# A Mamba and mixture-of-experts block: the chunk's diagonal products and C with B as two 64-column halves of the TensorE array

## The chip, the cores and the metric

One core of a Trainium2 chip runs the whole program in one launch. The metric is the device time of that launch in microseconds. Times below are from repeated executions and from one execution under the hardware profiler.

## The reference, cut to what matters

The input is 32 sequences of 512 tokens, 256 wide. Each goes through layer norm, a projection with rotary embedding, RMS norm, a state-space layer, layer norm and a residual; then through a feed-forward layer with a shared part and 16 experts, layer norm and a residual. The change lies in the state-space layer, whose state has 128 columns, with 8 heads of 64 channels each:

```python
Y_diag = jnp.einsum('bcln,bcsn,bhcls,bcshp->bclhp', Cr, Br, Lmat, xdt)
Y_off = jnp.einsum('bcln,bchpn,bhcl->bclhp', Cr, states_prev, jnp.exp(Acs))
return (Y_diag + Y_off).reshape(b, l, h, p)
```

`Y_diag` is what a token l receives from the tokens s of its own chunk: the product of C at l with B at s, times the decay from s to l, times the scaled input at s. `Y_off` is what it receives from the state left by the chunks before.

## The kernel before, in words

The kernel takes chunks of 128 tokens (the reference says 64; the recurrence gives the same sums), so a sequence has NT = 4 chunks. Everything is single precision. The large products (projections and the feed-forward layer) are written as three products of rounded parts, high x high, high x low and low x high, in the 32-bit rounded type (`split_mm`, whose matmul is L1443, and `down`, L1629). The products of the state-space layer are plain full-precision matmuls on unrounded data. Transposes are matmuls with the identity (L1452, L1462, L1608).

The program is software-pipelined over sequences: one pass of the loop does the state-space layer of one sequence and the feed-forward layer of the one before. Each engine runs a list of steps that is written out by hand: `lead`, `first`, `iteration(False)`, `iteration` in a loop of 29 passes, `tail`, `drain`, `last`. No planner works at run time. PSUM banks are handed out by the lists in `PLANS`: a group such as `"a"` has three banks that are used in turn, and `slot(name)` waits until the bank's last reader has freed it. `fill` marks the last matmul of a step with a semaphore increment.

The steps that matter here, all on TensorE:

- `CB()` (line 1541 on, matmul at L1547): once for each sequence. For each chunk t it makes B times C, a 128 x 128 matrix: 128 state rows are contracted, the stationary operand is `xc[:, 4, tk]` (B, 128 tokens), the moving one `xc[:, 5, tk]` (C, 128 tokens). The four results fill one bank; ScalarE copies them to `CBs` (L863).
- `diagonal(c)` (matmul at L1575): four times for each sequence. For each of the 8 heads h it multiplies the decayed and masked matrix `seg[:, c % 2, h, :]` (128 tokens s by 128 tokens l, stationary) with `xdt[:, c % 2, hs]` (128 tokens s by 64 channels, moving). It waits for `m_ready`, which VectorE gives when it has multiplied the decays by `CBs` (`decay_CB`, L1167). The eight results, 128 x 64 each, fill one bank; VectorE reads it in `chunk_y` (L1191 or, for the first chunk, L1193).
- `from_state(c)` (L1560) and `state(c)` (L1567): one full-precision matmul of 512 moving columns each.
- `cumulate()` (L1518, L1519, L1520): once for each sequence, three small full-precision matmuls on `ad`, the decays of 32 chunk-heads. L1518 and L1519 have 128 stationary and 32 moving columns. L1520 is the other way round: `rhs` with 32 columns is stationary, `upper` with 128 moves, and the result goes to partitions 0 to 31.
- `combine_by_expert()` (L1608): four transposes with 16 stationary columns.

The diagonals and `CB` stand between other steps in TensorE's order; in `iteration`:

```python
gate(4); CB(); x_by_token(0); up(3); down(1); x_by_token(1); combine_by_expert(); down(2)
settled("c_ready"); up(4); gate(5); state(0); project_z(3, 1); diagonal(0); up(5)
from_state(1); state(1); down(3); x_by_token(2); gate(6); diagonal(1); from_state(2); up(6)
```

In the profile a matmul is two kinds of record: the load of the stationary operand (PEld, LDWEIGHTS) and the stream of the moving one (PE, MATMUL). A full-precision `nc.tensor.matmul` shows as two pairs of load and matmul, a rounded-type one and a transpose as one pair.

Of the kernel before, what the change touches and what calls it, by code (L numbers as in the profile page):

```python
# [12 lines left out]
P = 128  # L13
# [19 lines left out]
def build(nc, x, wq_t, wzx_t, conv_w, conv_b, dt_bias, a_log, d_param, npw, ngw, wo_t,  # L33
# [6 lines left out]
    with ctx:  # L40
        def sb(name, shape, dt=fp32):
            return ctx.enter_context(nc.sbuf_tensor(name, shape, dt))
# [40 lines left out]
        xc = sb("xc", [P, CB_, T])  # L83
# [3 lines left out]
        xdt = sb("xdt", [P, 2, DI])  # L87
        xdec = sb("xdec", [P, 2, DI])
        xD, ysp = sb("xD", [P, 2, DI]), sb("ysp", [P, DI])
        seg = sb("seg", [P, 2, HS, P])  # L90
# [1316 lines left out]
        def _(pe):  # L1407
# [9 lines left out]
            def slot(name):  # L1417

                part, n = way.plan.where[name]
                w = len(BANKS[part])  # L1420
                if n >= w:
                    s, k = out_of(way.plan.slots[part][n - w][0], way.plan)
                    pe.wait_ge(sem[s], now(s, k) if SEM[s][3] else k)
                elif part != "p":
                    old = way.before if part in way.before.slots else way.plan
                    s, k = out_of([slot[0] for slot in old.slots[part][n::w]][-1], old)
                    pe.wait_ge(sem[s], k)
                return way.bank(name)

            def read_out(name):  # L1430
                s, k = out_of(name, way.plan)
                pe.wait_ge(sem[s], now(s, k) if SEM[s][3] else k)

            def fill(name, ins):
                part, n = way.plan.where[name]
                ins.then_inc(sem[f"{part}_for_{way.plan.slots[part][n][1]}"], 1)
# [104 lines left out]
            def CB():  # L1541
                b = slot("CB")
                read_out("xc4")
                read_out("xc5")
                for t in range(NT):
                    tk = slice(t * P, (t + 1) * P)
                    ins = nc.tensor.matmul(b[:, tk], xc[:, 4, tk], xc[:, 5, tk], start=True, stop=True)  # L1547
                fill("CB", ins)

            def x_by_token(c):  # L1550
# [18 lines left out]
            def diagonal(c):  # L1569
                b = slot(f"yd{c}")  # L1570
                read_out(f"xt{c}")
                pe.wait_ge(sem["m_ready"], c + 1)
                for h in range(HS):
                    hs = slice(h * PD, (h + 1) * PD)
                    ins = nc.tensor.matmul(b[:, hs], seg[:, c % 2, h, :], xdt[:, c % 2, hs], start=True, stop=True)  # L1575
                fill(f"yd{c}", ins)

            def y_by_channel(c):
# [80 lines left out]
            def first():  # L1659
                begin("first", "pa")  # L1660
                consts(); weights_split(1, 2); project_z(0, 0); project_z(0, 1); project_z(1, 0)
                project_z(2, 0); project_z(1, 1); project_z(3, 0); project_x(4); project_x(5); project_x(0)
                project_z(2, 1); project_x(1); cumulate(); project_x(2); settled("ad_ready"); project_x(3)
                project_z(3, 1); x_by_token(0); CB(); x_by_token(1); B_by_token(); state(0); diagonal(0)
                state(1); from_state(1); diagonal(1); x_by_token(2); from_state(2); state(2); x_by_channel(0)
                y_by_channel(0); diagonal(2); x_by_token(3); weights_split(3); project_out(0)
                settled("a_out_ACT", "xdec_ready"); y_by_channel(1); project_q(0); project_out(1)
                from_state(3); y_by_channel(2); x_by_channel(1); diagonal(3); project_q(1); settled("xn_ready")
                settled("m_ready"); project_out(2); settled("p_out_DVE"); y_by_channel(3); h_by_channel(0)
                project_out(3); settled("p_out_ACT"); settled("a_out_DVE", "yg_ready"); h_by_channel(1)  # L1670
                settled("qn_ready")
                weights_split(*range(4, len(SPLIT)))
                assert not open_

            def iteration(g=True):
                begin("steady", "paf" + g * "g")
                project_z(0, 0); project_z(1, 0); ffn_by_channel(0); project_x(4); ffn_by_channel(1)
                if g: down(10)
                settled("ffn_in_ready"); project_z(2, 0); project_x(5)
                if g: down(11); settled("last_split")  # L1680
                logits(0); logits(1); project_z(3, 0); project_x(0); gate(0); project_x(1); up(0); project_x(2)
                gate(1); up(1); project_z(0, 1); cumulate(); gate(2); settled("ad_ready"); project_z(1, 1)
                project_x(3); up(2); gate(3); down(0); settled("acc_free"); B_by_token(); project_z(2, 1)
# [3 lines that stand above are left out]
                down(4); y_by_channel(0); gate(7); state(2); up(7); settled("xdec_ready"); diagonal(2)  # L1687
                x_by_token(3); down(5); settled("a_out_ACT"); project_out(0); x_by_channel(0); y_by_channel(1)
                gate(8); from_state(3); project_q(0); project_out(1); down(6); up(8); y_by_channel(2)
                diagonal(3); down(7); settled("m_ready"); x_by_channel(1); gate(9); settled("xn_ready")  # L1690
                project_out(2); up(9); y_by_channel(3); project_q(1); settled("yg_ready"); down(8)
                settled("p_out_DVE"); project_out(3); gate(10); settled("a_out_DVE"); up(10); h_by_channel(0)
                down(9); settled("p_out_ACT"); settled("hidden_split"); gate(11); settled("f_out_ACT")
                h_by_channel(1); up(11); settled("f_out_DVE"); settled("qn_ready")
                assert not open_

            def tail():
                begin("tail", "afg")
                project_z(0, 0); ffn_by_channel(0); project_z(0, 1); project_x(4); ffn_by_channel(1); down(10)
                settled("ffn_in_ready"); project_x(5); down(11); settled("last_split"); project_z(1, 0)  # L1700
                logits(0); logits(1); project_x(0); gate(0); project_z(2, 0); up(0); project_z(3, 0); gate(1)
                project_x(1); up(1); project_x(2); gate(2); up(2); CB(); gate(3); cumulate(); down(0)
                settled("ad_ready"); settled("acc_free"); B_by_token(); project_z(1, 1); up(3); project_x(3)
                project_z(2, 1); down(1); combine_by_expert(); gate(4); settled("c_ready"); project_z(3, 1)
                up(4); x_by_token(0); gate(5); x_by_token(1); down(2); up(5); state(0); diagonal(0); state(1)
                from_state(1); gate(6); diagonal(1); down(3); y_by_channel(0); x_by_token(2); from_state(2)
                gate(7); x_by_token(3); up(6); settled("a_out_ACT"); down(4); state(2); diagonal(2)
                project_out(0); settled("xdec_ready"); up(7); down(5); y_by_channel(1); gate(8); from_state(3)
                up(8); project_out(1); down(6); gate(9); y_by_channel(2); diagonal(3); down(7)
                settled("m_ready"); up(9); project_out(2); gate(10); y_by_channel(3); down(8)  # L1710
                settled("yg_ready"); up(10); project_out(3); gate(11); settled("a_out_DVE")
                settled("f_out_ACT"); down(9); settled("hidden_split"); up(11); settled("f_out_DVE")
                assert not open_
# [77 lines left out]
```

## Time and profile before

| | |
|---|---|
| time, median of 3 runs | 3186.76 us (3184.94, 3186.76, 3191.86) |
| profiled execution, span from first to last instruction | 3185.9 us |
| PE (matmul) | 3112.3 us busy, 98%, 19648 matmuls |
| PEld (weight load) | 2722.1 us, 85% |
| DVE (VectorE) | 2394.2 us, 75% |
| POOL (GpSimd) | 2031.2 us, 64% |
| ACT (ScalarE) | 1935.2 us, 61% |
| mean granted TensorE clock | 0.989 of 2.4 GHz |

For the profiled execution only the span is given, 0.9 us under the median of the runs; its own device time is not listed beside it. Busy PE time overstates the work, since matmuls are pipelined and a record runs on while the next one has started: the length of a matmul record includes its way through the array. The distance from one start to the next is the better measure of what an instruction takes from the engine. In the timeline, instructions of one line that follow each other are merged into a row: its start, the time from the first start to the last end, and the count behind the x.

### The profile page before, as it was taken

The numbers are of one execution on the slowest core, as the hardware profiler recorded it, in microseconds if no ns is written. First come the engines' busy times: TensorE is split into PE (matmuls) and PEld (weight loads), VectorE is DVE, ScalarE is ACT, GpSimd is POOL, SyncE is SP. The second block draws the span as 40 slices with busy tenths as digits, with TensorE's granted clock in tenths as the row PEclk, the third lists the DMA queues.
The fourth block names the chain that finished last, engine by engine and source line by source line (L and its number), as shares of the span: only waits on it lengthen the run. The fifth ranks groups of instructions, "written<-read, shape, count | busy, mean of one in ns | idle before, by whom it ended". The sixth has DMA issues, their size and how long they took to land.

```text
span 3185.9 us, 62383 instructions
## 1 busy us (share of the span) xinstructions
PE 3112.3 (98%) x19648; PEld 2722.1 (85%) x19648; DVE 2394.2 (75%) x5104; ACT 1935.2 (61%) x4149; POOL 2031.2 (64%) x2311
## 2 busy tenths in 40 slices
PE   5899999999999999999999999999999999999997
PEld 4688888888888888888888888888888888888886
DVE  5877877777777777777777777778777777777763
ACT  5565666665666556666566666656656656665562
POOL 2477666677666676656676666776666776666764
PEclk7899999999999999999999999999999999999999
DMA  3123222222222222222122222222222222222222
GB/s 123 41 68 87 73 73 67 66 66 85 73 64 64 71 73 76 80 66 58 64 86 76 76 60 66 66 86 73 73 66 66 66 86 73 64 67 69 73 74 48
DMA packets 143433, 227.33 MB, mean 71 GB/s; under 512 B 18976, under 2 KB 88352, under 8 KB 143392
## 3 DMA queue, kind: packets, MB, share of 16 engines
q1 hardware_dynamic: 126496, 210.06, 20.1%
q0 software_dynamic: 16896, 16.78, 4.0%
q8 instruction: 20, 0.33, 0.0%
q14 instruction: 21, 0.17, 0.0%
HBM read 174.87 MB, written 35.13 MB: 66 GB/s over the span
## 4 chain that ended last, share of the span: by engine, by line
PE 95%; DVE 0%; POOL 0%; ACT 0%; issue 0%; ACTq 0%; DVEq 0%; POOLq 0%
PE fpb L1443 34%; PE apb L1443 20%; PE acc L1629 17%; PE apb L1575 7%; PE apb L1452 4%; PE ppb L1443 3%; PE apb L1560 3%; PE apb L1567 2%; PE ppb L1462 2%; PE apb L1547 1%; PE fpb L1492 1%; PE fpb L1462 1%; PE fpb L1494 1%; PE fpb L1608 0%; PE apb L1520 0%; PE apb L1519 0%
## 5 line engine op out<-in xcount | busy, mean ns | idle before, releaser
L652 POOL TENSOR_TENSOR hidL<-hid,hidH 128x512 fp32r<-128x512 f32 x384 | 544.9, 1419 | 234.8 <-ACT hidH L914 226.8
L1130 DVE SCALAR_TENSOR_TENSOR xc<-apb,cw,xc 128x511 f32<-128x511 f32 (+2 forms) x576 | 427.8, 747 | 63.9 <-ACT xc L827 35.9
L1629 PE MATMUL acc<-WDH,hidH 128*128 128x256 f32 x1536 | 456.7, 297 | 4.4 <-POOLq L654 4.4
L914 ACT CAST hidH<-hid 128x512 fp32r<-128x512 f32 x384 | 236.2, 615 | 341.9 <-POOL hid L647 283.6
L1629 PE MATMUL acc<-WDH,hidL 128*128 128x256 f32 x1536 | 431.4, 281 | 0.0
L1629 PE MATMUL acc<-WDL,hidH 128*128 128x256 f32 x1536 | 430.9, 281 | 0.0
L647 POOL TENSOR_TENSOR hid<-hid,cb 128x512 f32<-128x512 f32 x256 | 347.5, 1358 | 73.2 <-DVEq L1251 42.1
L1249 DVE TENSOR_TENSOR hid<-hid,fpb 128x512 f32<-128x512 f32 x384 | 261.1, 680 | 135.6 <-PE fpb L1443 132.3
L1443 PE MATMUL fpb<-fTh,UH 128*128 128x512 f32 x768 | 335.7, 437 | 0.0
L845 ACT ACTIVATE seg<-seg,acs 128x128 f32<-128x128 f32 x1024 | 313.6, 389 | 11.5 <-ACT cb L895 5.7
L1443 PE MATMUL fpb<-fTh,GH 128*128 128x512 f32 x768 | 318.6, 415 | 0.0
L1629 PEld LDWEIGHTS acc<-WDH,hidH 128*128 128x128 f32 x1536 | 289.9, 189 | 19.9 <-issue 7.4
L1443 PE MATMUL fpb<-fTh,GL 128*128 128x512 f32 x768 | 304.1, 396 | 0.0
L1443 PE MATMUL fpb<-fTh,UL 128*128 128x512 f32 x768 | 303.9, 396 | 0.0
L903 ACT ACTIVATE hid<-fpb 128x512 f32<-128x512 f32 x384 | 228.5, 595 | 123.2 <-PE fpb L1443 83.9
L1443 PE MATMUL fpb<-fTl,UH 128*128 128x512 f32 x768 | 302.5, 394 | 0.0
L1443 PE MATMUL fpb<-fTl,GH 128*128 128x512 f32 x768 | 302.5, 394 | 0.0
L1629 PEld LDWEIGHTS acc<-WDL,hidH 128*128 128x128 f32 x1536 | 290.1, 189 | 12.7 <-issue 7.2
L1629 PEld LDWEIGHTS acc<-WDH,hidL 128*128 128x128 f32 x1536 | 289.7, 189 | 0.0
L1575 PEld LDWEIGHTS apb<-xdt,seg 128*128 128x128 f32 x2048 | 246.7, 194 | 11.9 <-issue 6.6
L1575 PE MATMUL apb<-xdt,seg 128*128 128x64 f32 x2048 | 246.1, 274 | 2.9 <-DVE seg L1167 2.8
L1167 DVE TENSOR_TENSOR seg<-seg,CBs 128x1024 f32<-128x1024 f32 x128 | 198.4, 1550 | 43.6 <-ACT seg L845 34.1
(195 smaller groups left out, 8669.6 us busy)
## 6 DMA issues: line engine op xcount, KB each, us to landing
seg<-acs_row SPq DMA_DIRECT2D x128, 512.0 KB, 4.2
cb<-c_row SPq DMA_DIRECT2D x512, 128.0 KB, 2.9
xsP<-in_x SPq DMA_DIRECT2D x32, 512.0 KB, 3.6
xc<-qrot SPq DMA_DIRECT2D x32, 512.0 KB, 3.4
xc<-in_x SPq DMA_DIRECT2D x32, 512.0 KB, 4.3
out<-xc SPq DMA_DIRECT2D x32, 512.0 KB, 3.0
out<-xn POOLq DMA_DIRECT2D x32, 512.0 KB, 6.0
ZL_loaded<-in_wzx_t SPq DMA_DIRECT2D x2, 512.0 KB, 4.4
```

The lines of the kernel that those rows point to most:

```text
L647: G.tensor_tensor(hid[:, j % 2, :], hid[:, j % 2, :], cb[:, r % 2, :], ALU.mult).then_inc(sem["routed_ready"], 1)
L652: own.do(G.tensor_tensor(hidL[:, j % 2, :], hid[:, j % 2, :], hidH[:, j % 2, :].bitcast(fp32), ALU.subtract))
L845: ins = A.activation(seg[:, c % 2, h, :], seg[:, c % 2, h, :], ACT.Exp, bias=acs[:, 0, c * HS + h:c * HS + h + 1])
L903: own.do(A.activation(hid[:, j % 2, :], way.bank(f"G{j}")[:], ACT.Silu))
L914: A.copy(hidH[:, j % 2, :], hid[:, j % 2, :]).then_inc(sem["hidden_high"], 1)
L1130: ins = V.scalar_tensor_tensor(xc[:, b, s:], src[:, 0:T - s], cw[:, b, TAPS - 1 - s:TAPS - s], xc[:, b, s:], ALU.mult, ALU.add)
L1167: V.tensor_tensor(seg[:, c % 2, :, :], seg[:, c % 2, :, :], CBs[:, c, :].unsqueeze(1).broadcast_to([P, HS, P]), ALU.mult).then_inc(sem["m_ ...
L1249: own.do(V.tensor_tensor(hid[:, j % 2, :], hid[:, j % 2, :], way.bank(f"U{j}")[:], ALU.mult))
L1443: ins = nc.tensor.matmul(dst, l, r, start=n == 0, stop=n == total - 1)
L1452: ins = nc.tensor.transpose(b[:, t * P:(t + 1) * P], src(t), ident[:])
L1575: ins = nc.tensor.matmul(b[:, hs], seg[:, c % 2, h, :], xdt[:, c % 2, hs], start=True, stop=True)
L1629: ins = nc.tensor.matmul(dst, l[:, w, tk], r[:, j, :], start=j == 0 and t % 2 == 0 and n == 0, stop=j == HB - 1 and n == 2, skip_group_che ...
```

## The change

Each matmul of `CB` and of `diagonal` becomes two. The first takes the first 64 stationary columns and writes partitions 0 to 63 of the bank, the second takes the other 64 and writes partitions 64 to 127 in the same columns. The moving operand is the same for both. The semaphore increment of `fill` stays on the last matmul. Nothing else changes.

```diff
@@ CB
                 for t in range(NT):
                     tk = slice(t * P, (t + 1) * P)
-                    ins = nc.tensor.matmul(b[:, tk], xc[:, 4, tk], xc[:, 5, tk], start=True, stop=True)
+                    for r in range(0, P, P // 2):
+                        ins = nc.tensor.matmul(b[r:r + P // 2, tk], xc[:, 4, t * P + r:t * P + r + P // 2], xc[:, 5, tk],
+                                               start=True, stop=True)
                 fill("CB", ins)
@@ diagonal
                 for h in range(HS):
                     hs = slice(h * PD, (h + 1) * PD)
-                    ins = nc.tensor.matmul(b[:, hs], seg[:, c % 2, h, :], xdt[:, c % 2, hs], start=True, stop=True)
+                    for r in range(0, P, P // 2):
+                        rows_ = slice(r, r + P // 2)
+                        ins = nc.tensor.matmul(b[rows_, hs], seg[:, c % 2, h, rows_], xdt[:, c % 2, hs],
+                                               start=True, stop=True)
                 fill(f"yd{c}", ins)
```

## Rows read from the trace of the kernel before

**Rows 1.** The page: span, busy time and forty slices of TensorE, granted clock

```profile
span 3185.9 us, 62383 instructions
...
PE 3112.3 (98%) x19648; PEld 2722.1 (85%) x19648; DVE 2394.2 (75%) x5104; ACT 1935.2 (61%) x4149; POOL 2031.2 (64%) x2311
...
PE   5899999999999999999999999999999999999997
...
PEclk7899999999999999999999999999999999999999
```

**Rows 2.** The chain that ended last: by engine (page), then by line

```profile
PE 95%; DVE 0%; POOL 0%; ACT 0%; issue 0%; ACTq 0%; DVEq 0%; POOLq 0%
...
by line: PE fpb L1443 33.7%; PE apb L1443 19.5%; PE acc L1629 17.1%; PE apb L1575 6.7%; PE apb L1452 3.8%; PE ppb L1443 2.7%; PE apb L1560 2.5%; PE apb L1567 2.5%; PE ppb L1462 1.6%; PE apb L1547 0.9%; PE fpb L1492 0.9%; PE fpb L1462 0.8%; 
```

**Rows 3.** By source line: duration min/median/max, who waited; L1575, L1547, L1520

```profile
L1575 PE MATMUL apb<-xdt,seg x2048: 217/275/446, 70.6 to 3091.2; 128*128 128x64 f32 x187
...
  DVE xdt L1191: 85.4, 63
...
L1547 PE MATMUL apb<-xc x256: 270/275/423, 63.8 to 3039.0; 128*128 128x128 f32 x128
...
L1520 PEld LDWEIGHTS apb<-upper,ad x64: 105/108/153, 53.7 to 3041.0; 128*32 128x32 f32 x64
L1520 PE MATMUL apb<-upper,ad x64: 272/296/424, 53.7 to 3041.1; 128*32 128x128 f32 x64
```

**Rows 4.** Timeline of weight loads around one diagonal (start, length, count last)

```profile
1032.53 1.87 PEld L1575 LDWEIGHTS apb<-xdt,seg 128*128 128x128 f32 x16
1034.32 0.19 PEld L1443 LDWEIGHTS fpb<-fTh,UH 128*128 128x128 f32 x1
```

**Rows 5.** Timeline of matmuls, L1560

```profile
1035.83 1.02 PE L1560 MATMUL apb<-S,xc 128*128 128x512 f32 x2
```

**Rows 6.** Timeline of matmuls around one CB

```profile
1021.85 1.05 PE L1547 MATMUL apb<-xc 128*128 128x128 f32 x8
1022.74 0.60 PE L1452 MATMUL apb<-ident,xc 128*128 128x128 f32 x4
```

**Rows 7.** Timeline around L1520: matmuls, loads, loads in a late pass

```profile
1011.15 0.41 PE L1520 MATMUL apb<-upper,ad 128*32 128x128 f32 x2
1011.48 0.50 PE L1443 MATMUL fpb<-fTh,GH 128*128 128x512 f32 x1
1011.82 0.39 PE L1443 MATMUL fpb<-fTl,GH 128*128 128x512 f32 x1
...
1010.80 0.30 PEld L1519 LDWEIGHTS apb<-ad,ones 128*128 128x128 f32 x2
1011.14 0.14 PEld L1520 LDWEIGHTS apb<-upper,ad 128*32 128x32 f32 x2
1011.48 0.19 PEld L1443 LDWEIGHTS fpb<-fTh,GH 128*128 128x128 f32 x1 [0.20 <-issue]
...
2938.80 0.30 PEld L1519 LDWEIGHTS apb<-ad,ones 128*128 128x128 f32 x2
2939.14 0.14 PEld L1520 LDWEIGHTS apb<-upper,ad 128*32 128x32 f32 x2
2939.48 0.19 PEld L1443 LDWEIGHTS fpb<-fTh,GH 128*128 128x128 f32 x1 [0.20 <-issue]
```

**Rows 8.** Timeline around L1608: matmuls, then the load behind them

```profile
1025.98 0.60 PE L1452 MATMUL apb<-ident,xc 128*128 128x128 f32 x4
1026.41 0.60 PE L1608 MATMUL fpb<-ident,gt 128*16 128x128 f32 x4
...
1026.74 0.19 PEld L1629 LDWEIGHTS acc<-WDH,hidH 128*128 128x128 f32 x1
```

**Rows 9.** The chain in order of time: one product in two successive passes

```profile
1007.33 2.81 PE fpb L1443 x12
...
1103.73 2.81 PE fpb L1443 x12
```

## The prediction

> **What bounds the kernel now.** I read the page first: its busy shares and its forty slices [rows 1]. TensorE multiplies for 98% of the span, no other engine has over 75%, and the granted clock is at its upper level, 2.4 GHz, in nearly every slice. The chain that ended last [rows 2] says the same: 95% of it is PE, of which 6.7% of the span is L1575 (the products inside a chunk) and 0.9% is L1547 (C with B). TensorE is idle for 3185.9 - 3112.3 = 74 us, nearly all of it in the first, second and last slice [rows 1], outside the steady passes. So time added to TensorE's stream moves the end one for one, and time taken from it does so until a wait appears.
>
> What sets the pace in the two places is read from the timeline. A full-precision product is two records here: 2048 matmuls at L1575 for 1024 calls, 256 at L1547 for 128 calls [rows 3]. In one diagonal [rows 4] 16 weight loads start at 1032.53 and the next line's load at 1034.32: 1.79 us, 0.112 each. The matmul of 64 moving columns needs less. From the two 512-column matmuls of L1560 [rows 5], whose starts lie 1.02 - 0.60 = 0.42 us apart, a full-precision column costs 0.82 ns, so 64 of them 0.053 us and 128 of them 0.106. L1575 is therefore **bound by weight loads** (0.112 against 0.053), and half of its streaming time is idle. CB [rows 6] runs 8 matmuls from 1021.85 to 1022.74, 0.111 each, with load and stream in balance.
>
> **The change part by part.** All waits, semaphores, buffers and the order stay. Every call becomes two calls with 64 stationary columns, one writing PSUM partitions 0 to 63 and one 64 to 127. A diagonal goes from 16 pairs (load and matmul) to 32, a CB from 8 to 16; over 32 sequences that is 128 diagonals and 32 CBs, 2048 + 256 more pairs. No DMA is added, and none of VectorE, ScalarE or GpSimd gets another instruction.
>
> *One pair.* A load of 128 columns takes 0.112 us. The only short load in a matmul of this kind is that of L1520, 32 columns [rows 3, 7]: two of them span 0.14 us and one is recorded at 0.108, so they start 0.03 us apart. Load time goes by columns, and 64 columns cost about 0.057. The stream of 64 moving columns is 0.053, that of 128 is 0.106. Both halves stream all moving columns again.
>
> *Entering and leaving.* L1520 is also the only product of this kernel that uses a part of the columns with ordinary matmuls, and its surroundings are not smooth [rows 7]. The loads of L1519 start at 1010.80 and, at 0.112 each, end at 1011.02; their last matmul streams 32 columns, 0.03 us; yet L1520's load starts only at 1011.14: **0.09 us in which nothing loads or streams**. Behind it: the second matmul starts at 1011.15 + 0.41 - 0.27 = 1011.29 (0.27 is the length of L1520's shortest matmul [rows 3]), streams 128 columns until 1011.39, and the next line's load starts at 1011.48, 0.09 us later. That load isn't hidden either: the matmul that needs it is recorded with 0.50 us instead of 0.39, 0.11 more. The same distances stand around L1520 in every pass of the loop; the last one is beside it [rows 7]. They don't stand around L1608, whose stationary operand has 16 columns but which is a transpose [rows 8]: its first matmul starts 0.43 us after the first of L1452's four, and the load of L1629 follows 0.33 us behind it, 0.11 for each of three. I take it that the array changes its division between L1519 and L1520 and back, and that each change waits until it is empty. The Trainium skill (TensorEngine Tiling (Array Packing), Key Properties) says that changing the tiling mode drains TensorE, and (Restrictions) that column tiling excludes 32-bit transposes; the trace agrees with both.
>
> No two of the 160 groups are neighbours in any of the orders written out, so each pays both changes: 0.095 empty, 0.057 for a first load that nothing covers, then at the end 0.095 and 0.11.
>
> *The body.* Here the trace has no row: nowhere do two instructions address different column halves. The bounds are (a) nothing of the two halves overlaps, (b) loads follow each other but streams may run side by side, (c) loads and streams of the halves both run side by side. With the passes in the order A1 A2 B1 B2, (c) pairs A2 with B1 and B2 with the next A1, so that n products take 2n + 1 steps.
> - Diagonal, (a) or (b): 32 x 0.057 = 1.82. With the ends 0.095 + 0.057 + 1.82 + 0.095 + 0.11 = 2.18 against 1.79: +0.39, times 128 = **+50 us**.
> - Diagonal, (c): 17 x 0.057 = 0.97, with the ends 1.33: -0.46, times 128 = -59 us.
> - CB, (b) or (c): streams of 0.111 side by side, 9 x 0.111 = 1.00, with the ends 1.36 against 0.89: +0.47, times 32 = **+15 us**.
> - CB, (a): 16 x 0.111 = 1.78, with the ends 2.13: +1.24, times 32 = +40 us.
>
> I take (b), and keep (a) and (c) as ends: every row shows loads one after another, back to back, at a rate that goes by columns alone, as one supply of weights would; the streams are the part of the array that a half leaves free. The halves' loads together still bring 2 x 64 = 128 columns a pass, which is what L1575 is bound by now. That would be -59 us where I put +50 if loads ran side by side.
>
> The Trainium skill is of two minds here. TensorE: Matmul & The Clock Gate (Weight-path perf modes) gives a wider weight path no gain for fp32, which speaks for one supply, while its page TensorEngine Tiling (Array Packing) (Key Properties) says that different tiles can execute LdWeights and Matmul in parallel. By the first the sum is +65, by the second -44. No run here shows either.
>
> *What else moves.* VectorE waits for the end of a diagonal in 63 places at L1191 alone (85 us together [rows 3]) and gets it 0.4 us later; what TensorE waits for from there (the gated y) comes after other matmuls that are just as much later, so I cost this at nothing. If that cover were gone it would be up to 0.4 us a chunk. The clock stays at its upper level: the gaps are 0.1 us, and L1520's do not change it.
>
> **Sum.** 50 + 15 = +65 us, +2.0%. The profiled execution spans 3185.9 us, 0.9 below the median of 3186.8, so I add to the median: **3252 us**. What a measurement of this kernel can tell from no change is about 0.2%, 6 us.
>
> **Rivals.**
> - *(a) Nothing overlaps*: 50 + 40, 3277 us. For it: no row has two matmuls streaming at once. Against: a half-wide stream leaves the other half of the array free. Chance 0.22.
> - *(c) The halves load and stream side by side*: -59 + 15 = -44, **3143 us**. This is the mechanism of the other sign: L1575 is load-bound, and two half loads at once cut its pace from 0.112 to 0.057 a pass. It wins as soon as the 32 pairs take less than 1.79 - 0.36 for the ends - 0.12 for a diagonal's share of CB's 15 us = 1.31 us, that is under 0.041 us a pair; above that the two changes of the array's division eat it. For it: half of the streaming time at L1575 is idle now, and the halves have no cell in common. Against: the rate of loads in every row. Some of the gain may come back as waits, since VectorE and GpSimd have 64 to 75% and 1.4 us fewer a pass to hide in. Chance 0.30.
> - *A pair of a diagonal costs 0.11 after all*, because in the divided array a load is not hidden by a matmul (0.057 + 0.053), or because TensorE isn't handed two instructions in less than the 0.111 us that are the shortest steady distance now. CB's pair costs 0.057 + 0.111. With the ends that is +2.2 and +2.1 us a group: 3530 us. Against: L1520's second load starts 0.03 us after the first, under its matmul, and its two matmuls follow at the pace of streaming alone [rows 7]. Chance 0.05. The Trainium skill (TensorE: Matmul & The Clock Gate, Packing small matmuls) has a load overlap running matmuls only where the row groups differ, and the two halves share all rows; L1520 speaks against that.
> - *The array is not emptied* (as with L1608): a diagonal then costs 1.82 + 0.057 against 1.79, and the time is 3187 to 3200. Against: L1520 in every pass. Chance 0.07.
> - The forecast (b): chance 0.36.
>
> **How the numbers follow.** 3252 is the case (b), the likeliest. Slower by over 0.2% holds (b), (a), the third and a part of the fourth: 0.66. Faster is (c): 0.30. Within 0.2%: 0.04, from the fourth. Both signs have weight, so the range reaches from (c) to (a) with a few us for the sizes of the gaps: 3138 to 3290; it leaves out the 3530 us and a (c) whose streams gain more. Given (b) alone it is 3235 to 3265: the gaps are known to 0.01 us each, 160 x 0.03, and a pair's 0.057 to 0.002, 4096 x 0.002 = 8 us.
>
> **What would show it.** In the changed profile a diagonal is one block of 32 loads of 128 rows x 64 columns, about 1.82 us from its first load to its last matmul in (b) and (a), 0.97 in (c); a CB of 16 matmuls spans 1.0 us in (b) and 1.8 in (a). Before each block the loads stop for about 0.1 us, and the first matmul behind each is 0.11 us longer than its kind, which the forms of L1443, L1452 and L1629 show in their means. The share of L1575 in the chain rises from 6.7%, and TensorE's idle time outside these gaps stays near 74 us. The prediction is wrong if a pair of a diagonal takes well under 0.05 us, if no gap stands around the blocks, or if a pass of the loop (96.4 us now, by the starts of the rows of the same kind in successive passes [rows 9]) is not about 2 us longer.

## The result and the profile after

The changed kernel takes 3138.6 us (median of 4 runs, 3134.3 to 3140.8) against 3186.6 us before: a ratio of 0.9843, with a 95% interval from 0.9829 to 0.9857. It is **1.6% faster**, 48 us, where 2.0% slower was forecast. The profiled execution of the changed kernel took 3134.3 us and spans 3132.6, 53.3 us less than that of before.

The page of the changed kernel and, last, its chain by line (as [rows 1, 2]):

```profile
span 3132.6 us, 66991 instructions
...
PE 3056.3 (98%) x21952; PEld 2615.7 (83%) x21952; DVE 2359.2 (75%) x5104; ACT 1932.0 (62%) x4149; POOL 2033.6 (65%) x2311
...
PE 94%; POOL 1%; DVE 0%; ACT 0%; issue 0%; DMA 0%; SPq 0%; ACTq 0%; POOLq 0%; DVEq 0%
...
by line: PE fpb L1443 34.1%; PE apb L1443 19.7%; PE acc L1634 17.4%; PE apb L1579 4.2%; PE apb L1452 4.1%; PE ppb L1443 2.7%; PE apb L1562 2.7%; PE apb L1569 2.5%; PE ppb L1462 1.7%; PE apb L1548 1.0%; PE fpb L1492 0.9%; PE fpb L1494 0.9%; 
```

TensorE has 2304 pairs more and is busy for 56 us less; it is still the bound. The diagonals (now L1579) fell from 6.7% to 4.2% of the chain. Their block is read from the timeline of the loads, then of the matmuls, in the changed kernel:

```profile
1013.06 0.19 PEld L1443 LDWEIGHTS apb<-ZH,hTl 128*128 128x128 f32 x1
1013.38 1.01 PEld L1579 LDWEIGHTS apb<-xdt,seg 128*64 128x64 f32 x32
1014.46 0.19 PEld L1443 LDWEIGHTS fpb<-fTh,UH 128*128 128x128 f32 x1
1014.57 0.19 PEld L1443 LDWEIGHTS fpb<-fTl,UH 128*128 128x128 f32 x1
...
1013.38 1.15 PE L1579 MATMUL apb<-xdt,seg 128*64 128x64 f32 x32
1014.46 0.50 PE L1443 MATMUL fpb<-fTh,UH 128*128 128x512 f32 x1
```

From the first load to the next line's load the block takes 1.08 us for **32** pairs; before, it took 1.79 us for 16 [rows 4]. Of the 1.08, 0.055 is the first load, 0.09 the empty time at the end, and the rest, 0.93, is 16 steps of 0.058: two pairs a step. The price of the change of mode is those two terms and one more ahead of the block: the last full load starts at 1013.06 and the first half load 0.32 later, not 0.12. These 0.20 us more are 0.09 in which nothing loads or streams, and 0.11 in which the last full matmul streams with no load under it. Behind the block the first load is not hidden, and its matmul is recorded with 0.50 us, but before the change it was recorded with 0.48 in the same place (the second row below): that load costs little more than it did. To compare whole detours, I take the distance from the last full load ahead of the block to the second load behind it. Before, around the same diagonal (with the matmul behind it) and around CB:

```profile
1032.41 0.19 PEld L1443 LDWEIGHTS apb<-ZH,hTl 128*128 128x128 f32 x1
...
1034.35 0.48 PE L1443 MATMUL fpb<-fTh,UH 128*128 128x512 f32 x1
...
1034.43 0.19 PEld L1443 LDWEIGHTS fpb<-fTl,UH 128*128 128x128 f32 x1
...
1021.39 0.19 PEld L1443 LDWEIGHTS fpb<-fTh,GL 128*128 128x128 f32 x1
...
1023.07 0.19 PEld L1443 LDWEIGHTS fpb<-fTh,UH 128*128 128x128 f32 x1
```

and around CB in the changed kernel (loads):

```profile
1001.73 0.19 PEld L1443 LDWEIGHTS fpb<-fTh,GL 128*128 128x128 f32 x1
1002.28 0.85 PEld L1548 LDWEIGHTS apb<-xc 128*64 128x64 f32 x16 [0.36 <-issue]
...
1003.69 0.19 PEld L1443 LDWEIGHTS fpb<-fTh,UH 128*128 128x128 f32 x1
```

A diagonal went from 2.02 to 1.51 us, **-0.51**. CB, with the four transposes behind it, went from 1.68 to 1.96, **+0.28**: its 16 pairs run two at a time as well, but a step there is the stream of 128 moving columns, 0.109 us against 0.111 before, and the change of mode comes on top. 4 x -0.51 + 0.28 = -1.76 us a pass. The passes, by the start of L1520's load in two of them (loads of the changed kernel),

```profile
896.72 0.14 PEld L1520 LDWEIGHTS apb<-upper,ad 128*32 128x32 f32 x2
...
991.49 0.14 PEld L1520 LDWEIGHTS apb<-upper,ad 128*32 128x32 f32 x2
```

take 94.77 us against 96.40 [rows 9]: -1.63, or 51 us over 31. Laid load by load beside the pass of the kernel before, the four diagonals give -0.50 each (-2.01) and CB +0.31 by the time the next diagonal starts; the last 0.07 is small shifts in between.

### The profile page after: what moved, and what is told of

It reads as the page before. It is cut to its first block, busy times and chain, and to the rows that moved or that the text cites. A ratio compares the mean times of both kernels' runs of the same rounds, so it can differ in the third digit from the quotient of the medians.

```text
span 3132.6 us, 66991 instructions
## 1 busy us (share of the span) xinstructions
PE 3056.3 (98%) x21952; PEld 2615.7 (83%) x21952; DVE 2359.2 (75%) x5104; ACT 1932.0 (62%) x4149; POOL 2033.6 (65%) x2311
## 4 chain that ended last, share of the span: by engine, by line
PE 94%; POOL 1%; DVE 0%; ACT 0%; issue 0%; DMA 0%; SPq 0%; ACTq 0%; POOLq 0%; DVEq 0%
PE fpb L1443 34%; PE apb L1443 20%; PE acc L1634 17%; PE apb L1579 4%; PE apb L1452 4%; PE ppb L1443 3%; PE apb L1562 3%; PE apb L1569 2%; PE ppb L1462 2%; PE apb L1548 1%; PE fpb L1492 1%; PE fpb L1494 1%; PE fpb L1462 1%; PE fpb L1613 0%; PE apb L1520 0%
## 5 line engine op out<-in xcount | busy, mean ns | idle before, releaser
L622 POOL TENSOR_TENSOR xD<-xD,xdt 128x512 f32<-128x512 f32 x128 | 210.3, 1643 | 24.0 <-DVEq L1196 24.0
L827 ACT ACTIVATE xc<-apb,cbv,cw 128x512 f32<-128x512 f32 x192 | 149.1, 777 | 110.1 <-PE apb L1443 65.9
L1167 DVE TENSOR_TENSOR seg<-seg,CBs 128x1024 f32<-128x1024 f32 x128 | 164.7, 1287 | 52.3 <-ACT seg L845 42.8
```

Source lines behind the costliest of these rows:

```text
L622: own.do(G.tensor_tensor(xD[:, c % 2, :], xD[:, c % 2, :], xdt[:, c % 2, :], ALU.add))
L827: A.activation(xc[:, b, :], way.bank(f"xc{b}")[:], ACT.Identity, bias=cbv[:, b:b + 1], scale=cw[:, b, TAPS - 1:TAPS]).then_inc(sem["conv_f ...
L1167: V.tensor_tensor(seg[:, c % 2, :, :], seg[:, c % 2, :, :], CBs[:, c, :].unsqueeze(1).broadcast_to([P, HS, P]), ALU.mult).then_inc(sem["m_ ...
```

## The experiments

Each was run beside the kernel before on the same chip; ratios are to that. The first diff is against the changed kernel, the others against the first experiment, `diag_only`. Diffs are cut to the lines that matter; `...` stands for what is left out.

**diag_only and cb_only: one half of the change each.** `diag_only` leaves L1547 as it was; `cb_only` leaves L1575 as it was.

```diff
-  for r in range(0, P, P // 2):
-      ins = nc.tensor.matmul(b[r:r + P // 2, tk], xc[:, 4, t * P + r:t * P + r + P // 2], xc[:, 5, tk], ...)
+  ins = nc.tensor.matmul(b[:, tk], xc[:, 4, tk], xc[:, 5, tk], start=True, stop=True)
```

> CB is whole again, the diagonals stay in halves. Theory 1 (two halves load and stream at once, and each block of halves pays for emptying the array before and behind it): in the changed kernel CB took 1.17 us from the end of the stream before it to the next full-pace matmul where it took 0.89 before, so undoing it gives back 0.28 us x 32 = 9 us: about 3129 us. Theory 2 (the halves of CB save time too): slower than the changed kernel, 3145 us or more.

> Only CB is in halves. Theory 1: a loss of 0.28 us x 32 = 9 us against the kernel before, about 3196 us. Theory 2: a gain, 3180 us or less.

Measured: `diag_only` 0.9834 (0.982 to 0.9848), `cb_only` 1.004 (1.0025 to 1.0054), 13 us slower than before with the interval from 8 to 17. The halves of CB cost time when they stand alone, as Theory 1 says. Undoing them in the changed kernel should give 9 us back; 0.9834 against 0.9843 is 3 us, inside the intervals. The passes show where about 5 of the 9 went (loads of `diag_only`; the last row is from an earlier pass of the long kind):

```profile
897.81 0.14 PEld L1520 LDWEIGHTS apb<-upper,ad 128*32 128x32 f32 x2
...
992.65 0.14 PEld L1520 LDWEIGHTS apb<-upper,ad 128*32 128x32 f32 x2
...
1087.11 0.14 PEld L1520 LDWEIGHTS apb<-upper,ad 128*32 128x32 f32 x2
...
595.04 0.19 PEld L1632 LDWEIGHTS acc<-WDH,hidH 128*128 128x128 f32 x1 [0.30 <-POOLq L654]
```

One pass takes 94.84 us, the next 94.46. The short kind is the 0.3 us less that Theory 1 expects; the long kind, 12 of the 29 in the loop, has TensorE waiting at the start of the pass for the low part of a hidden product, which GpSimd makes (last row). Those 12 passes have this wait, and none of the short ones has it. The chain that ended last in `diag_only` says that GpSimd has come to the edge:

```profile
PE 73%; POOL 19%; issue 2%; DMA 1%; DVE 1%; ACT 0%; POOLq 0%; SPq 0%; DVEq 0%; ACTq 0%
```

**not_alternating: all of one half, then all of the other.**

```diff
-  for h in range(HS):
-      hs = slice(h * PD, (h + 1) * PD)
-      for r in range(0, P, P // 2):
+  for r in range(0, P, P // 2):
+      for h in range(HS):
+          hs = slice(h * PD, (h + 1) * PD)
...
```

> CB whole; in a diagonal all eight heads of the upper half are done first, then all eight of the lower, the same 32 pairs in another order. Theory 1: neighbours now share a half, nothing can run beside anything, a pair costs 0.057 us, the block 1.8 us, and with the emptying a diagonal costs 0.39 us more than before: 3186.6 + 50 = about 3237 us. Theory 3 (TensorE takes later instructions forward over several others, or a 64-column pair costs 0.03 us by itself): the order does not matter, 3129 us as with the diagonals alone.

Measured 1.0098 (1.0084 to 1.0113), 31 us slower than before and 84 us slower than the same 32 pairs in alternation. The loads around one diagonal in `not_alternating`:

```profile
1041.98 0.19 PEld L1443 LDWEIGHTS apb<-ZH,hTl 128*128 128x128 f32 x1
1042.31 1.76 PEld L1577 LDWEIGHTS apb<-xdt,seg 128*64 128x64 f32 x32
1044.14 0.19 PEld L1443 LDWEIGHTS fpb<-fTh,UH 128*128 128x128 f32 x1
1044.24 0.19 PEld L1443 LDWEIGHTS fpb<-fTl,UH 128*128 128x128 f32 x1
```

The gain is in the alternation, not in the narrow loads: Theory 3 falls. The block takes 1.83 us, and the detour is 2.26 against 2.02 before, +0.24. Both are less than 32 pairs in a row would make: 0.055 + 32 x 0.058 + 0.09 = 2.00. Three steps of 0.058 are missing, although only one pair of neighbours lies in different halves. So the lower half has begun while two passes of the upper were still to start. The single records, which the row merges, agree: first a load starts every 0.055 to 0.059 us, then three times two loads start within 0.005 us (1043.06, 1043.12 and 1043.17), then single ones follow again.

**by_twos and by_fours: how far ahead?** The heads in groups of two or four: a group's upper halves, then its lower halves.

```diff
-  for h in range(HS):
-      for r in range(0, P, P // 2):
+  for h, r in [(g + i, r) for g in range(0, HS, 2) for r in range(0, P, P // 2) for i in range(2)]:
```

> CB whole; in a diagonal two heads of the upper half, the same two of the lower, then the next two heads: four passes of one half, four of the other. In not_alternating the lower half began while two passes of the upper were still to start. Theory 7 (a pass of the other half can start over up to two waiting passes of this half): only the first pass of a block stands alone, 16 or 17 steps of 0.058, the block about 1.14 us from its first load to the next line's. Theory 8 (strictly in order): only neighbours overlap, 25 steps, about 1.6 us.

> The same with four heads at a time: eight passes of one half, eight of the other, twice. Theory 7: three passes overlap at each of the three changes of side, 32 - 9 = 23 steps, about 1.45 us a block. Theory 8: one at each, 29 steps, about 1.8 us.

The loads of one diagonal in `by_twos`:

```profile
1013.87 1.06 PEld L1575 LDWEIGHTS apb<-xdt,seg 128*64 128x64 f32 x32
1015.00 0.19 PEld L1443 LDWEIGHTS fpb<-fTh,UH 128*128 128x128 f32 x1
```

and in `by_fours`:

```profile
1025.45 1.40 PEld L1575 LDWEIGHTS apb<-xdt,seg 128*64 128x64 f32 x32
...
1026.93 0.19 PEld L1443 LDWEIGHTS fpb<-fTh,UH 128*128 128x128 f32 x1
```

1.13 and 1.48 us, where Theory 7 had 1.14 and 1.45 and strict order 1.6 and 1.8. A pass starts over up to two waiting ones of the other half. Each was run once, 3136.3 us and 3173.3. That `by_twos` is no slower than `diag_only`, with blocks 0.05 us longer, goes with its passes: all in the loop take 94.65 us, none 94.84, so the 0.2 us that its blocks cost are about what `diag_only` loses to the wait.

**one_full_head: the price of the change of mode.**

```diff
+  w = P if h == 4 else P // 2
-  for r in range(0, P, P // 2):
-      rows_ = slice(r, r + P // 2)
+  for r in range(0, P, w):
+      rows_ = slice(r, r + w)
...
```

> CB whole; in a diagonal the fifth of eight heads is done with full 128 columns, the others in halves, so each diagonal leaves and enters the divided state once more. Theory 1: the detour costs 0.09 + 0.11 + 0.11 + 0.06 + 0.09 + 0.05 = 0.52 us for two passes that took 0.12 in halves: +0.40 us x 128 = +51 us against the diagonals alone, about 3180 us. Theory 4 (the gaps around a block come from something else than the change between halves and whole): only the longer loads count, 0.22 - 0.12 = 0.11 us x 128 = 14 us, about 3143 us.

Measured 0.9956 (0.9941 to 0.9972), 39 us more than `diag_only` by the ratios. The loads of one diagonal in `one_full_head`, 28 of halves and 2 of full width in one row:

```profile
1028.49 1.41 PEld L1578 LDWEIGHTS apb<-xdt,seg 128*64 128x64 f32 x30
1029.96 0.19 PEld L1443 LDWEIGHTS fpb<-fTh,UH 128*128 128x128 f32 x1
```

The block is 1.47 instead of 1.08: +0.39, against the 0.40 expected and the 0.11 of Theory 4. So the gaps come from leaving and entering the divided state. (By the ratios the whole is 10 us short of 128 x 0.39 = 50. Its passes all take 95.97 us, and `diag_only` has 0.4 us of waiting in 12 of its own, some 5 us of these.)

**rest_first: is it GpSimd's order?**

```diff
-  combine(11); rest(10); rest(11)
+  rest(10); combine(11); rest(11)
```

> As the diagonals alone, and GpSimd's list ends with the low part of the eleventh hidden product ahead of the last multiplication by the routing weights (they had the other order). In the run with the diagonals alone about half of the passes take 94.84 us instead of 94.45, and the 0.4 us are lost where TensorE waits for that low part (0.30 us, GpSimd). Theory 5 (GpSimd at the end of the pass has become the bound that cuts the gain): every pass takes 94.45, some 6 us less than with the diagonals alone, about 0.982 of the kernel before. Theory 6 (the 0.4 us come from elsewhere or move to the next hidden product): 94.84 in the same share of passes, or more, and no gain.

Measured 1.0091 (1.0077 to 1.0104), 82 us slower than `diag_only` by the ratios. Theory 5's remedy fails: the passes take 96.6 or 98.1 us, not 94.45. The wait moved and grew, as Theory 6 allows and as the longest line of TensorE's waits in `rest_first` shows:

```profile
PE apb L1443 <- ACT zs L855: 58.9, 31, 2.0
```

In this order the last multiplication waits behind the low part, ScalarE's rounding waits for it, and ScalarE comes later to z (L855), whose bank the next pass of TensorE then waits for. That the 0.4 us are a wait on GpSimd is read from the trace, and not shown by a run that removes it.

`after_again` was the changed kernel beside these:

> The changed kernel once more, beside the next two on one chip. Theory 1: its passes of the loop take 94.76 us as in its profile, the diagonals alone should take 0.3 us less a pass, so it is some 9 us slower than rest_first and 0 to 9 us slower than the diagonals alone.

It gave 0.9838 (0.9824 to 0.9851), not separable from `diag_only` (0.9834, on another chip).

**cumulate_halves: do the loads overlap, or only the streams?** The products L1518 and L1519 move only 32 columns.

```diff
-  nc.tensor.matmul(b[:, 0:n], upper[:], rhs, start=True, stop=True)
-  nc.tensor.matmul(b[:, n:2 * n], ones[:], rhs, start=True, stop=True)
+  for w, cs in ((upper, slice(0, n)), (ones, slice(n, 2 * n))):
+      for r in range(0, P, P // 2):
+          nc.tensor.matmul(b[r:r + P // 2, cs], w[:, r:r + P // 2], rhs, start=True, stop=True)
```

> CB whole, diagonals in halves, and the first two products of cumulate in halves too (128 stationary columns, 32 moving): their stream is 0.027 us, so only the loads set the pace. Theory 1 (the two halves really load at the same time): 8 pairs in 4 steps of 0.057. Theory 9 (the halves only stream side by side, and their loads alternate): each load of 64 columns takes 0.055 of its own, 8 x 0.055 = 0.44 us. Behind them stands the product with 32 stationary columns: if going from halves to a narrower part empties the array too, its load starts 0.09 us after the last stream, otherwise at once.

Loads of `cumulate_halves`:

```profile
1085.31 0.20 PEld L1520 LDWEIGHTS apb<-ad,upper 128*64 128x64 f32 x4
1085.42 0.20 PEld L1520 LDWEIGHTS apb<-ad,ones 128*64 128x64 f32 x4
1085.66 0.14 PEld L1521 LDWEIGHTS apb<-upper,ad 128*32 128x32 f32 x2
```

The second four loads start 0.11 us after the first four: 4 x 64 columns in 0.11 us, where one after another, at the 0.055 of Theory 9, they need 0.22. This pace alone leaves a rival: loads or streams that follow each other at 0.027 us each, evenly. How many records are under way in short stretches tells the two apart (`cumulate_halves`, L1520; start and end, length, then matmuls and loads, each busy with its count, then clock and DMA):

```profile
1085.30:1085.32 0.02, 0.01 (x2) 0.01 (x2) 1.00 0.00 0
1085.32:1085.36 0.04, 0.04 (x2) 0.04 (x2) 1.00 0.00 0
1085.36:1085.38 0.02, 0.02 (x2) 0.02 (x4) 1.00 0.00 0
```

Two loads have begun by 1085.32, none is added in the next 0.04 us, then two more: they start in twos, 0.007 us apart, a new two every 0.055 to 0.058. The 32 loads of a diagonal in the changed kernel start in the same twos. So **both halves load at once**; Theory 9 falls, and the rival too. Going on from 64 to 32 columns costs an empty time too, 0.10 us: four steps from 1085.31 would have the last stream end at 1085.56, and the next load starts at 1085.66.

As this version had the shortest time of all, it was timed beside the changed kernel on one chip:

> CB whole, diagonals and the first two products of cumulate in halves, now timed. Theory 1: its passes take 94.44 us against 94.77 of the changed kernel, 31 x 0.33 = 10 us or 0.3% less than the changed kernel beside it, about 0.981 of the kernel before. Theory 2 (CB in halves costs nothing that reaches the end): no difference to the changed kernel.

> The changed kernel beside it on the same chip: 0.984 of the kernel before, passes of 94.77 us.

0.9815 (0.9801 to 0.983) against 0.9849 (0.9835 to 0.9864). The intervals do not touch: CB whole, and diagonals and cumulate in halves, is 0.3% faster than the changed kernel beside it. Its passes, by two loads of `cumulate_timed`, take 94.43 us, as the short ones of `diag_only` do, so the halves of cumulate give next to nothing themselves (0.2 us of loads, less one more change of mode). What is gained is that all passes but one are of the short kind; why the wait on GpSimd is gone here is not settled, and `diag_only` was not timed on this chip:

```profile
895.56 0.14 PEld L1521 LDWEIGHTS apb<-upper,ad 128*32 128x32 f32 x2
...
989.99 0.14 PEld L1521 LDWEIGHTS apb<-upper,ad 128*32 128x32 f32 x2
```

**quarters: four parts of 32 columns.**

```diff
-  for r in range(0, P, P // 2):
-      rows_ = slice(r, r + P // 2)
+  for r in range(0, P, P // 4):
+      rows_ = slice(r, r + P // 4)
```

> CB whole; in a diagonal each head is four products of 32 columns instead of two of 64, 64 pairs. A load is 0.028 us, a stream still 0.053. Theory 7 (a pass can start over at most two waiting ones, each part has its own load and stream): at least two, at most four parts run at once, so a head takes two steps if all four do (block about 1.1 us) and about 1.5 to 2.0 us a block if only two or three do. Theory 10 (TensorE is handed instructions at no more than one in 0.027 us, which halves do not reach: 4 in 0.058): 128 instructions take 3.4 us, slower than before the change.

Loads of one diagonal in `quarters`:

```profile
1055.52 0.94 PEld L1577 LDWEIGHTS apb<-xdt,seg 128*32 128x32 f32 x64
1056.55 0.19 PEld L1443 LDWEIGHTS fpb<-fTh,UH 128*128 128x128 f32 x1
```

64 pairs in 1.03 us, four at a time, and no limit of issue in sight: Theory 10 falls, and the block is even 0.05 shorter than in halves. (Its 3.4 us, 0.027 for each of 128 instructions, were excluded before this run: in halves 64 instructions take 1.08 us, 0.017 each. Counted by pair it gives 64 x 0.027 = 1.7 us, which this run excludes.) Yet the single run took 3281.5 us, 146 more than `diag_only` on another chip. The time is lost at the start of each pass. The page of `quarters` (queue of instruction fetches: packets, MB), then its two longest waits of TensorE, and then TensorE in a stretch of 4 us behind such a start:

```profile
q8 instruction: 278, 4.55, 0.6%
...
PE apb L1443 <- issue: 69.4, 28, 2.9
PE apb L1443 <- PEq L1530: 44.3, 30, 3.5
...
1010.00:1014.00 4.00, 3.24 (x16) 3.19 (x16) 0.33 (x2) 0.00 (x0) 1.49 (x2) 0.57 0.01 4
```

The queue that brings instructions moved 22 packets in `diag_only` and moves 278 here, some 9 more for each pass of the loop, and TensorE waits 114 us for its own stream. Behind the wait the granted clock is at 1.2 GHz for part of the time (0.57 on average in that stretch). So the loop, with 25792 pairs in the whole execution instead of 21696, seems no longer to stay on the core and is fetched again in each pass. At which size this begins was not tried.

## Why the prediction was wrong

- **What bounds the kernel**: right. TensorE's stream was the path, and L1575 was bound by its loads.
- **Entering and leaving**: right in size. L1520's gaps carried over: 0.09 us empty, and 0.11 for a stream and a load that do not overlap. In a diagonal the ends come to 0.34 where the sum had 0.36, but the 0.11 is lost ahead of the block, not behind it, where the first load was exposed before as well (0.48 against 0.50). `one_full_head` priced a detour at 0.39 where these terms made 0.40. Behind CB the exposed load is that of a transpose and shorter, about 0.06.
- **The step that failed is "I take (b)"**, that the loads of the two halves follow each other. The changed kernel and `cumulate_halves` show that they run at the same time: the 32 pairs of a diagonal take 16 steps of 0.058 us, 0.93, where (b) had 32 steps of 0.057, 1.82. The argument was that every row shows loads one after another. But every such row is of full-width matmuls or of the same columns; it said nothing on two halves. The absence of a row was taken for evidence. The rule on fp32 weights that was set beside it (the Trainium skill, TensorE: Matmul & The Clock Gate, Weight-path perf modes) is on one load being split, not on two loads; the sentence that did bear on the case is the other one of the Trainium skill (TensorEngine Tiling (Array Packing), Key Properties), and the trace agrees with it. With the +50 us of the diagonals the sign fell too: 128 x -0.51 = -65 us. Two of the signs that the prediction named for being wrong are there: a pair takes 0.029 us, and a pass is 1.63 us shorter instead of 2 longer.
- **The rival (c)** named the mechanism, and its 3143 us are 4 us off, which is in part luck. Both of its terms were too dear: -0.46 a diagonal, measured -0.51, and +0.47 a CB, measured +0.28. With the measured terms its sum is -65 + 9 = -56 us, not -44; the kernel gained 48. The extra step of "2n + 1" is in both (0.06 and 0.11): there is none, since the first two halves start together. In CB the exposed load behind the block was also put too high.
- **The third rival**, a pair at 0.11 us, has its two prices in the wrong order: 32 x 0.11 + 0.36 - 1.79 = +2.1 us a diagonal, and 16 x 0.168 + 0.36 - 0.89 = +2.2 a CB. Its 3530 us stand, and a pair at 0.029 excludes them.
- **Serial pairs** were put at +0.39 a diagonal; `not_alternating` has +0.24, the three steps that overlap at the change of side.
- **"A wait appears"** was named as what may eat a gain and given no price. In the changed kernel it costs next to nothing; in `diag_only` it takes 0.4 us in 12 of 29 passes, and in `cumulate_halves`, with passes as short, in next to none. What decides that is open.

## What to carry to other kernels

Where a matmul has 128 stationary columns and 64 moving ones in full precision, as here, its pace is that of the load, and two products of 64 columns, in alternation, halve it: 0.116 us a call instead of 0.22. A block pays about 0.34 us once (0.09 empty twice, and at either end a load and a stream that do not overlap; 8 calls x 0.106 - 0.51), so it takes some four calls to gain, and products whose stream is as long as their load only lose. A resource that no row shows in use by two at once is unknown, not excluded; such a term decides a sign, and belongs with a chance that says so.

## What the runs showed that was not expected

- Passes of one half start over up to two waiting passes of the other: blocks of 1.13, 1.48 and 1.83 us for groups of two, four and eight heads, each within 0.03 of that count. This takes the order of the kernel's calls to be the order in which TensorE gets them. The Trainium skill (TensorE: Matmul & The Clock Gate, Packing small matmuls) has matmuls start strictly in order; if that held, these blocks would be 1.6, 1.8 and 1.95.
- Four quarters load and stream at once as well: 64 pairs in 1.03 us.
- A loop of TensorE that grew by a fifth was, by its packets, fetched again in each pass: 278 packets instead of 22, and 146 us.
